# A gather of 1,563 tiles of rows: SyncE and ScalarE no longer fetch fifteen of them, GpSimd does

## The chip, the cores and the metric

The kernel runs on one core of a Trainium2 chip. The metric is the device time of one execution, in microseconds (us), as the median of several runs.

## What is computed

One layer of a graph network over N = 12,500 nodes with D = 256 features and E = 200,000 edges (src, dst), the edges sorted by dst:

```python
h = relu(layernorm(x))                      # per node, over 256 features
agg = segment_sum(h[src], dst, N)           # 200,000 gathered rows of 1 KB
t = ((1 + eps) * h + agg) @ W1 + b1         # W1 256 x 512
t = relu(batchnorm(t))                      # over all nodes
out = x + relu(batchnorm(t @ W2 + b2 + h))  # W2 512 x 256
```

All data are fp32.

## The kernel before

The edges are cut into 1,563 tiles of 128 (`TILES`), and these into 196 groups of `GT` = 8 (`NG`). For a tile, 128 rows of 1 KB are gathered from DRAM into 128 partitions; for a group, VectorE builds selection matrices (`selection`, `h_step`), and TensorE multiplies and sums them over the tiles of the group into a window of 96 nodes (`aggregate`, L1324). The window is copied, transposed and added into `aggT`.

In groups 0 to 29 (`H_FROM` = 30) the rows come from `x`, and VectorE and ScalarE normalise every gathered row (`statistics`, `normalise`). Beside this, all nodes are normalised once in batches of 512 and stored in DRAM as `h_rows`; from group 30 on the rows come from there and need no more work. Behind this, node tiles go through `z_tile` and `times_W1`. After the last group the kernel computes the first batch norm, multiplies by W2 (`times_W2`, L1442), computes the second batch norm, transposes back and adds x (`transpose_out`, L1456).

The order on each engine is written out by hand. GpSimd's program is a list of gathers, one indirect DMA for a tile (`gather`, L650):

```python
if g >= RG:
    pool.wait_ge(s_agg, g - RG + 1)      # RG = 4 buffers: group g - 4 must be aggregated
for k in range(tiles_of(g)):
    if sp_tile(g, k) or act_tile(g, k):
        continue
```

Fifteen tiles are left out there. SyncE fetches the last tile of groups 26, 54, 76, 96, 118, 140, 160 and 182 (`sp_groups`; group 26 from x), and ScalarE the last but one of groups 54, 75, 96, 118, 139, 160 and 182 (`act_groups`). Each does so with 128 DMAs of one row (`load_rows`, L512 and L1197), in pieces of 16, long before the group comes. For this each engine loads the byte offsets of the rows into registers. The offsets come from a table in DRAM (`row_at`): ScalarE multiplies the src table by 1,024 (L1078), SyncE stores it (L518), and GpSimd waits for that store (`s_atd`) before group 2, since the gathers' own table is made in the same place. Three buffers of rows for SyncE lie in `rl_odd`, three for ScalarE in `W2s`; therefore W2 is loaded only after ScalarE's last tile has been used (L566), and TensorE waits for it at L1433.

TensorE's wait at the head of a group (`wait_rows`) counts GpSimd's rows, and in the groups named also SyncE's and ScalarE's.

Of the kernel before, what the change touches and what calls it, by code (L numbers as in the profile page):

```python
# [39 lines left out]
SP_EIGHTHS = 6  # L40
ACT_EIGHTHS = 3
# [7 lines left out]
ROW_BUFS = 3  # L49
PIECE = 16  # L50
AT_ONCE = 32
QUAD = 4
ROW_BYTES = 4 * D


def ceil(a, b):
    return -(-a // b)


def build(nc, x, src, dst, W1, b1, g1, bt1, W2, b2, g2, bt2, eps_gin, out):  # L60
# [25 lines left out]
    with ctx:  # L86
# [6 lines left out]
        at_dram = nc.dram_tensor("row_at", (EB, P, P), i32, kind="Internal").ap()  # L93
        x_bytes = x.rearrange("n d -> (n d)").bitcast(mybir.dt.uint8)

        h_dram = nc.dram_tensor("h_rows", (N, D), f32, kind="Internal").ap()
        h_bytes = h_dram.rearrange("n d -> (n d)").bitcast(mybir.dt.uint8)
        H_ACT = H_FROM - 1

        def eighths(q, n):  # L100
            return q * n // 8

        per_tile = P // PIECE
        sp_groups = []
        while True:
            done = ceil(8 * per_tile * (len(sp_groups) + 1), SP_EIGHTHS)
            if done > H_NODES or 2 * (done - 1) + 6 >= H_FROM:
                break
            sp_groups.append(2 * (done - 1) + 6)
        SP_X = len(sp_groups)  # L110
        while True:
            done = ceil(8 * per_tile * (len(sp_groups) - SP_X + 1), SP_EIGHTHS) + H_NODES
            if 2 * (done - 1) + 6 >= NG - 4:
                break
            sp_groups.append(2 * (done - 1) + 6)

        act_groups = []
        while True:
            done = ceil(8 * per_tile * (len(act_groups) + 1), ACT_EIGHTHS) + H_ACT
            if done - 1 + 4 >= NG - 4:  # L120
                break
            act_groups.append(done - 1 + 4)

# [84 lines left out]
        assert COPIES_FROM % 2 == 1 and COPIES_FROM > max(H_ACT, 2 * H_NODES + 2, NQ + 2)  # L208
# [8 lines left out]
        sp_rows = [rl_odd[:, b * D:(b + 1) * D] for b in range(ROW_BUFS)]  # L217
        sp_at = [rl_odd[0:1, ROW_BUFS * D + b * P:ROW_BUFS * D + (b + 1) * P].bitcast(i32) for b in (0, 1)]
        w2_early = W2s.rearrange("p f d -> p (f d)")
        act_rows = [w2_early[:, b * D:(b + 1) * D] for b in range(ROW_BUFS)]  # L220
        act_at = [w2_early[0:1, ROW_BUFS * D + b * P:ROW_BUFS * D + (b + 1) * P].bitcast(i32) for b in (0, 1)]
# [40 lines left out]
        s_sprows = [sem(f"s_sprows{b}") for b in range(ROW_BUFS)]  # L262
        s_actrows = [sem(f"s_actrows{b}") for b in range(ROW_BUFS)]
        s_actat = [sem(f"s_actat{b}") for b in (0, 1)]
        s_spat = [sem(f"s_spat{b}") for b in (0, 1)]
        s_at, s_atd = sem("s_at"), sem("s_atd")
# [34 lines left out]
        def sp_tile(g, k):  # L301

            return g in sp_groups and k == GT - 1

        def act_tile(g, k):

            return g in act_groups and k == GT - 2

# [3 lines left out]

        def pool_tiles(g):

            return sum(not sp_tile(g, k) and not act_tile(g, k) for k in range(tiles_of(g)))
# [5 lines left out]
        def rows_of(g, k):  # L321
            if sp_tile(g, k):
                return sp_rows[sp_groups.index(g) % ROW_BUFS]
            if act_tile(g, k):
                return act_rows[act_groups.index(g) % ROW_BUFS]
            return rows[slot(g)][:, k, :]

        def row_pieces(first, end, tiles):

            return [divmod(n, P // PIECE) for n in range(first, min(end, tiles * P // PIECE))]  # L330

# [32 lines left out]
        def wait_rows(eng, g):  # L364

            eng.wait_ge(s_rows[g % RG], 16 * sum(pool_tiles(j) for j in range(g % RG, g + 1, RG)))
            if g in sp_groups:
                j = sp_groups.index(g)
                eng.wait_ge(s_sprows[j % ROW_BUFS], 16 * P * (j // ROW_BUFS + 1))
            if g in act_groups:  # L370
                j = act_groups.index(g)
                eng.wait_ge(s_actrows[j % ROW_BUFS], 16 * P * (j // ROW_BUFS + 1))

        def tiles_of(g):

            return min(GT, TILES - g * GT)
# [51 lines left out]
        def _(sp):  # L428
# [24 lines left out]
            sp.dma_start(W1s[:, :, :], W1.rearrange("(k p) n -> p k n", p=P)).then_inc(s_w, 16)  # L453

# [35 lines left out]
            def load_at(j):  # L490
                b, p = divmod(sp_groups[j] * GT + GT - 1, P)
                sp.dma_start(sp_at[j % 2], at_dram[b, p:p + 1, :]).then_inc(s_spat[j % 2], 16)

            row_regs = []

            def load_rows(j, m):
                if m == 0:
                    if j + 1 < len(sp_groups):
                        load_at(j + 1)
                    if j >= ROW_BUFS:  # L500
                        sp.wait_ge(s_agg, sp_groups[j - ROW_BUFS] + 1)
                    sp.wait_ge(s_spat[j % 2], 16 * (j // 2 + 1))
                if m * PIECE % AT_ONCE == 0:
                    regs = [sp.alloc_register(f"row{j}_{m}_{k}") for k in range(AT_ONCE)]
                    sp.reg_load(regs, sp_at[j % 2][0:1, m * PIECE:m * PIECE + AT_ONCE])
                    row_regs.extend(regs)
                for k in range(PIECE):
                    e = m * PIECE + k
                    reg = row_regs.pop(0)
                    at = sp.snap(reg, donate=True, min_val=0, max_val=(N - 1) * ROW_BYTES)  # L510
                    a = x_bytes if j < SP_X else h_bytes
                    sp.dma_start(sp_rows[j % ROW_BUFS][e:e + 1, :].bitcast(mybir.dt.uint8),  # L512
                                 a[bass.ds(at, ROW_BYTES)].rearrange("(p e) -> p e", p=1)
                                 ).then_inc(s_sprows[j % ROW_BUFS], 16)
                    sp.free_register(reg)

            sp.wait_ge(s_at, 1)
            sp.dma_start(at_dram.rearrange("b p e -> p b e"), tab_i[0]).then_inc(s_atd, 16)  # L518
            def pieces_of_pass(c):

                if c < H_NODES:
                    return row_pieces(eighths(SP_EIGHTHS, c), eighths(SP_EIGHTHS, c + 1), SP_X)
                c -= H_NODES
                return [(SP_X + j, m) for j, m in row_pieces(eighths(SP_EIGHTHS, c), eighths(SP_EIGHTHS, c + 1),
                                                            len(sp_groups) - SP_X)]

# [9 lines left out]
            for c in range(NT):  # L536
# [18 lines left out]
                if c == 0:  # L555
                    sp.wait_ge(s_trc[0], NTR)
                    sp.wait_ge(s_trc[1], NTR)
                    for b in (2, 3):
                        sp.dma_start(hb[b], batch_nodes(x, b, 0, P)).then_inc(s_pl[b], 16)
                    sp.wait_ge(s_atd, 16)  # L560
                    load_at(0)
                for j, m in pieces_of_pass(c):
                    load_rows(j, m)

            sp.wait_ge(s_agg, act_groups[-1] + 1)
            sp.dma_start(W2s[:, :, :], W2.rearrange("(k p) n -> p k n", p=P)).then_inc(s_w, 16)  # L566
# [53 lines left out]
        def _(pool):  # L620
# [11 lines left out]
            def gather(g):  # L632
                if g == PG:
                    pool.wait_ge(s_trc[1], NTR)
                    wait_apart(pool, s_trc[0], NTR)
                    wait_apart(pool, s_atd, 16)
# [4 lines left out]
                for k in range(tiles_of(g)):  # L641
                    if sp_tile(g, k) or act_tile(g, k):
                        continue
# [423 lines left out]
        def _(act):  # L1067
# [9 lines left out]
            act.wait_ge(s_tabf[0], 1)  # L1077
            S.activation(tab_i[0], tab_f[0], ACT.Copy, scale=float(ROW_BYTES)).then_inc(s_at, 1)  # L1078
# [97 lines left out]
            def load_at(j):  # L1176
                b, p = divmod(act_groups[j] * GT + GT - 2, P)
                act.dma_start(act_at[j % 2], at_dram[b, p:p + 1, :]).then_inc(s_actat[j % 2], 16)

            row_regs = []  # L1180

            def load_rows(j, m):
                if m == 0:
                    if j + 1 < len(act_groups):
                        load_at(j + 1)
                    if j >= ROW_BUFS:
                        act.wait_ge(s_agg, act_groups[j - ROW_BUFS] + 1)
                    act.wait_ge(s_actat[j % 2], 16 * (j // 2 + 1))
                if m * PIECE % AT_ONCE == 0:
                    regs = [act.alloc_register(f"act_row{j}_{m}_{k}") for k in range(AT_ONCE)]  # L1190
                    act.reg_load(regs, act_at[j % 2][0:1, m * PIECE:m * PIECE + AT_ONCE])
                    row_regs.extend(regs)
# [11 lines left out]
            def step(g):  # L1204
# [8 lines left out]
                if g == H_ACT:  # L1213
                    wait_h(act)
# [269 lines left out]
```

## Time and profile before

| What | Value |
|---|---|
| Median of 3 runs | 2167.27 us (2165.49 to 2168.1) |
| The profiled execution's own time | 2164.91 us |
| Its span, first to last instruction | 2163.1 us |
| GpSimd (POOL) busy | 1465.6 us, 68% of the span |
| TensorE (PE) busy | 1439.7 us, 67% |
| VectorE (DVE), ScalarE (ACT) busy | 769.0 and 338.3 us |
| Mean granted TensorE clock | 0.827 of full speed |
| DMA traffic | 324.90 MB, 150 GB/s over the span |

The own time is 1.81 us longer than the span: what lies around the instructions. Busy time leaves out the instructions that move registers, wait or issue a DMA on the hardware queues; a gather on GpSimd is counted for the part in which the engine works on it.

### The profile page before, as it was taken

What the parts mean: (1) busy time and instruction counts of PE and PEld (TensorE: products, weight loads), DVE (VectorE), ACT (ScalarE), POOL (GpSimd) and SP (SyncE); (2) the same over time, 40 slices, a digit from 0 to 9 for tenths busy, and PEclk for the clock granted to TensorE, in tenths of its full rate; (3) what the DMA queues carried; (4) which work ended last, traced back from release to release, by engine and by line L of the source; (5) the groups of instructions that cost most, each with busy time, mean ns of one, the idle gap of its engine ahead of it and who ended that gap; (6) DMA issues with size and microseconds to landing.
All of it is one profiled execution on the core that took longest, in us unless ns stands there. A gap on an engine that the chain in (4) does not pass through costs nothing.

```text
span 2163.1 us, 19306 instructions
## 1 busy us (share of the span) xinstructions
PE 1439.7 (67%) x4835; PEld 916.7 (42%) x4835; DVE 769.0 (36%) x1947; ACT 338.3 (16%) x661; POOL 1465.6 (68%) x1558
## 2 busy tenths in 40 slices
PE   3556667666665656575666575665666565689998
PEld 2334444444443434343444343433444343454446
DVE  7776753222322321322222222222232232134447
ACT  6667660000000000000000000000000000014446
POOL 7777777777777777777777777777777777760000
PEclk7788788787887877888778878888787788799999
DMA  6666654434434434434434443443443443448438
GB/s 201 214 226 213 223 170 128 138 109 135 137 108 135 135 116 128 135 115 128 136 115 125 138 122 119 135 136 106 135 135 106 135 134 115 144 126 320 178 139 317
DMA packets 119738, 324.90 MB, mean 150 GB/s; under 512 B 30146, under 2 KB 50939, under 8 KB 113487
## 3 DMA queue, kind: packets, MB, share of 16 engines
q0 software_dynamic: 74304, 203.00, 31.7%
q1 hardware_dynamic: 37036, 96.28, 12.5%
q10 hardware_dynamic: 8290, 24.43, 3.3%
q8 instruction: 38, 0.62, 0.1%
q14 instruction: 70, 0.57, 0.1%
HBM read 271.54 MB, written 52.05 MB: 150 GB/s over the span
## 4 chain that ended last, share of the span: by engine, by line
POOL 65%; issue 21%; PE 11%; DMA 1%; ACT 0%; DVE 0%; SPq 0%; DVEq 0%; POOLq 0%
POOL arena L650 65%; PE ps L1442 8%; PE ps L1456 1%; PE ps L1324 1%; DMA arena<-h_rows,arena 1%; PE ps L1360 0%; PE ps L1398 0%; DMA arena<-in_src 0%; DVE arena L1057 0%; SPq L439 0%; ACT aggT L1072 0%; ACT arena L1078 0%; ACT arena L1076 0%; PE ps L1334 0%; SPq L433 0%
## 5 line engine op out<-in xcount | busy, mean ns | idle before, releaser
L650 POOL DMA_INDIRECT arena<-h_rows,arena x1309 | 1237.4, 945 | 398.8 <-issue 397.9
L1324 PE MATMUL ps<-arena 128*96 128x256 f32 x3096 | 992.6, 491 | 688.2 <-DMA arena<-h_rows,arena 564.6
L1324 PEld LDWEIGHTS ps<-arena 128*96 128x96 f32 x3096 | 652.8, 217 | 1012.9 <-issue 748.4
L840 DVE TENSOR_TENSOR aggT<-aggT,ps 128x192 f32 x196 | 69.4, 354 | 1104.1 <-PE ps L1334 1101.7
L1151 ACT COPY arena<-ps 96x256 f32<-96x256 f32 x37 | 13.3, 358 | 1605.3 <-PE ps L1334 1570.0
L650 POOL DMA_INDIRECT arena<-in_x,arena x223 | 211.0, 946 | 67.9 <-issue 67.6
L1360 PE MATMUL ps<-arena 128*128 128x512 f32 (+3 forms) x412 | 186.3, 577 | 1.6 <-DVE arena L873 1.5
L1442 PE MATMUL ps<-arena,W2s 128*128 128x512 f32 (+1 forms) x400 | 167.9, 582 | 0.8 <-ACT arena L1272 0.8
L927 DVE TENSOR_TENSOR arena<-arena,ps 128x768 f32<-128x768 f32 x159 | 149.8, 942 | 0.0
L1103 ACT ACTIVATE arena<-arena,nb,mv 128x256 f32<-128x256 f32 x239 | 120.7, 587 | 84.5 <-DVE nb L744 84.5
L1442 PEld LDWEIGHTS ps<-arena,W2s 128*128 128x128 f32 x400 | 75.8, 190 | 92.8 <-issue 86.3
L676 DVE BATCH_NORM_STATS2 st<-arena 128x6 f32<-128x256 f32 x239 | 80.9, 411 | 58.6 <-DMA arena<-in_x,arena 58.5
L1360 PEld LDWEIGHTS ps<-arena 128*128 128x128 f32 x412 | 69.6, 190 | 48.1 <-issue 44.5
L924 DVE TENSOR_SCALAR arena<-ps,prmT 128x512 f32<-128x512 f32 x79 | 59.3, 751 | 75.9 <-PE ps L1360 75.9
L1272 ACT ACTIVATE arena<-arena,sh,sc 128x512 f32<-128x512 f32 (+1 forms) x100 | 72.1, 793 | 89.9 <-PE ps L1442 79.8
L1035 DVE SCALAR_TENSOR_TENSOR aggT<-ps,prmT,aggT 128x512 f32<-128x512 f32 (+1 forms) x50 | 36.9, 738 | 95.5 <-PE ps L1442 95.5
L1334 PEld LDWEIGHTS ps<-ident,arena 96*128 96x128 f32 x392 | 55.2, 142 | 26.5 <-ACT arena L1151 1.2
L918 DVE COPY arena<-ps 96x256 f32<-96x256 f32 x159 | 65.8, 414 | 0.1
L1334 PE MATMUL ps<-ident,arena 96*128 96x96 f32 x392 | 64.9, 246 | 0.6 <-ACT arena L1151 0.5
L881 DVE BATCH_NORM_STATS2 arena<-arena 128x6 f32<-128x512 f32 x92 | 63.0, 685 | 3.9 <-ACT arena L1160 3.9
L1117 ACT ACTIVATE arena<-arena,pnb,pmv 128x256 f32<-128x256 f32 (+1 forms) x100 | 51.7, 592 | 0.0
L934 DVE SCALAR_TENSOR_TENSOR arena<-ps,eps,aggT 128x256 f32<-128x256 f32 x80 | 38.1, 476 | 0.0
(99 smaller groups left out, 553.4 us busy)
## 6 DMA issues: line engine op xcount, KB each, us to landing
t_T<-arena SPq DMA_DIRECT2D x24, 1024.0 KB, 4.6
arena<-t_T SPq DMA_DIRECT2D x24, 1024.0 KB, 4.8
arena<-h_rows,arena POOLq DMA_INDIRECT x1309, 2.8
rl_odd<-h_rows SPq DMA_DIRECT2D x896, 1.0 KB
W2s<-h_rows ACTq DMA_DIRECT2D x896, 1.0 KB
arena<-in_x SPq DMA_DIRECT2D x27, 512.0 KB, 5.9
h_rows<-arena ACTq DMA_DIRECT2D x24, 512.0 KB, 3.7
out<-arena SPq DMA_DIRECT2D x23, 512.0 KB
```

The lines of the kernel that those rows point to most:

```text
L650: nc.gpsimd.indirect_dma_start(out=rows[slot(g)][:, k, :], out_offset=None, in_=(x if g < H_FROM else h_dram)[:, :], in_offset=bass.Indire ...
L676: last = V.bn_stats(o, r)
L840: V.tensor_tensor(z, z, winT_ps, ALU.add).then_inc(s_add, 1)
L881: V.bn_stats(o, t[:, m, :]).then_inc(s_tst, 1)
L918: V.tensor_copy(win_sb[g % 2], win_ps[g % 2]).then_inc(s_ev, 1)
L927: V.tensor_tensor(sel[:, g % 2, :, :], rel[:, g * GT:(g + 1) * GT].unsqueeze(2).to_broadcast([P, GT, W]), iota_ps.unsqueeze(1).to_broadcas ...
L1103: last = S.activation(rows_of(g, k), rows_of(g, k), ACT.Relu, bias=nb[:, g % 2, k:k + 1], scale=mv[:, g % 2, k, 1:2])
L1272: S.activation(u[:, k % 2, f, 0:n], tin[:, k % 2, f, 0:n], ACT.Relu, bias=sh1[:, f:f + 1], scale=sc1[:, f:f + 1]).then_inc(s_u, 1)
L1324: last = T.matmul(win_ps[g % 2], sel[:, g % 2, k, :], rows_of(g, k), start=k == 0, stop=k == n - 1)
L1334: last = T.transpose(winT_ps[:, f, :], win_sb[w % 2][:, f * P:(f + 1) * P], ident[0:W, 0:W])
L1360: last = T.matmul(t_ps[(FB * q + m) % TB][:, a:b], W1s[:, k, m * P:(m + 1) * P], zt[q % 2][:, k, a:b], start=k == 0, stop=k == DB - 1)
L1442: last = T.matmul(c_ps[k % 2][m][:, 0:n], W2s[:, f, m * P:(m + 1) * P], u[:, k % 2, f, 0:n], start=f == 0, stop=f == FB - 1)
```

## The change

The change takes out the fetches by SyncE and ScalarE with all that served them: the lists of groups, the offsets table and its store, the row buffers, their semaphores, and GpSimd's wait for `s_atd`. GpSimd gathers the fifteen tiles in their place in its order. W2 is loaded straight after W1, and TensorE waits for both before its first group. The waits of the remaining code are, as before, attached to the next instruction of their engine.

```diff
@@ wait_rows
-            eng.wait_ge(s_rows[g % RG], 16 * sum(pool_tiles(j) for j in range(g % RG, g + 1, RG)))
-            if g in sp_groups:
-                j = sp_groups.index(g)
-                eng.wait_ge(s_sprows[j % ROW_BUFS], 16 * P * (j // ROW_BUFS + 1))
-            if g in act_groups:
-                j = act_groups.index(g)
-                eng.wait_ge(s_actrows[j % ROW_BUFS], 16 * P * (j // ROW_BUFS + 1))
+            eng.wait_ge(s_rows[g % RG], 16 * sum(tiles_of(j) for j in range(g % RG, g + 1, RG)))
@@ SyncE
             sp.dma_start(W1s[:, :, :], W1.rearrange("(k p) n -> p k n", p=P)).then_inc(s_w, 16)
+            sp.dma_start(W2s[:, :, :], W2.rearrange("(k p) n -> p k n", p=P)).then_inc(s_w, 16)
...
-            sp.wait_ge(s_at, 1)
-            sp.dma_start(at_dram.rearrange("b p e -> p b e"), tab_i[0]).then_inc(s_atd, 16)
...
-                for j, m in pieces_of_pass(c):
-                    load_rows(j, m)
-
-            sp.wait_ge(s_agg, act_groups[-1] + 1)
-            sp.dma_start(W2s[:, :, :], W2.rearrange("(k p) n -> p k n", p=P)).then_inc(s_w, 16)
@@ GpSimd, gather
                     wait_apart(pool, s_trc[0], NTR)
-                    wait_apart(pool, s_atd, 16)
...
                 for k in range(tiles_of(g)):
-                    if sp_tile(g, k) or act_tile(g, k):
-                        continue
@@ ScalarE
             S.copy(tab_f[0], tab_i[0]).then_inc(s_tabf[0], 1)
-            act.wait_ge(s_tabf[0], 1)
-            S.activation(tab_i[0], tab_f[0], ACT.Copy, scale=float(ROW_BYTES)).then_inc(s_at, 1)
...
-                if g == H_ACT:
-                    wait_h(act)
-                if g >= H_ACT:
-                    for j, m in row_pieces(eighths(ACT_EIGHTHS, g - H_ACT), eighths(ACT_EIGHTHS, g - H_ACT + 1),
-                                           len(act_groups)):
-                        load_rows(j, m)
@@ TensorE
-            pe.wait_ge(s_w, 16)
+            pe.wait_ge(s_w, 32)
...
-            pe.wait_ge(s_w, 32)
```

GpSimd's list around group 54, before (a row is the group's first gather with its wait, or its other gathers; `arena` holds the gathered rows):

```order
L650 DMA arena<-h_rows,arena 128x256 x7
L650 DMA arena<-h_rows,arena 128x256 [waits s_agg]
L650 DMA arena<-h_rows,arena 128x256 x5
L650 DMA arena<-h_rows,arena 128x256 [waits s_agg]
L650 DMA arena<-h_rows,arena 128x256 x7
```

The same place now:

```order
L533 DMA arena<-h_rows,arena 128x256 x7
L533 DMA arena<-h_rows,arena 128x256 [waits s_agg]
L533 DMA arena<-h_rows,arena 128x256 x7
L533 DMA arena<-h_rows,arena 128x256 [waits s_agg]
L533 DMA arena<-h_rows,arena 128x256 x7
```

Group 54 had six gathers and has eight; where only SyncE or only ScalarE had a tile, x6 became x7.

SyncE's list at the outset, before (W1 and W2 both print as `in_L_gnn_W`):

```order
L452 DMA arena<-in_x 128x1024 x2
L453 DMA arena<-in_L_gnn_W 128x2x512
L518 DMA row_at<-arena 128x13x128 [waits s_at]
L460 DMA arena<-in_x 128x256
L559 DMA arena<-in_x 128x1024 [waits s_trc_dst,s_trc_src]
L559 DMA arena<-in_x 128x1024
L492 DMA rl_odd<-row_at 1x128 [waits s_atd]
```

The same place now:

```order
L380 DMA arena<-in_x 128x1024 x2
L381 DMA arena<-in_L_gnn_W 128x2x512
L382 DMA W2s<-in_L_gnn_W 128x4x256
L389 DMA arena<-in_x 128x256
L451 DMA arena<-in_x 128x1024 [waits s_trc_dst,s_trc_src]
L451 DMA arena<-in_x 128x1024
```

W2's load stands where the store of the offsets stood, and waits for nothing; the first node tile behind it no longer has a wait ahead of it.

## Rows read from the trace of the kernel before

**Rows 1.** The page, part 4: the chain of work that ended last.
```profile
POOL 65%; issue 21%; PE 11%; DMA 1%; ACT 0%; DVE 0%; SPq 0%; DVEq 0%; POOLq 0%
```
**Rows 2.** All gathers of line 650: durations (ns min/median/max), starts, idle time before.
```profile
L650 POOL DMA_INDIRECT arena<-h_rows,arena x1309: 942/946/958, 303.1 to 1938.1; - x187
L650 POOL DMA_INDIRECT arena<-in_x,arena x223: 942/946/1004, 24.2 to 301.9; - x112
L650 POOL DMA_INDIRECT arena<-in_x,idx x16: 942/946/1176, 3.8 to 22.9; - x16
...
  issue: 469.8, 1542
  DMA idx<-in_src: 1.3, 1
  PE ps L1324: 1.2, 4
  DVE arena L722: 0.3, 1
```
**Rows 3.** Busy time by stretch: start:end length, engines (instructions), PEclk, DMA share, GB/s.
```profile
600.00:800.00 200.00, 124.33 (x421) 81.30 (x422) 53.79 (x102) 0.00 (x0) 151.23 (x161) 0.81 0.41 122
...
1960.00:2020.00 60.00, 60.00 (x141) 26.60 (x140) 25.47 (x36) 26.36 (x36) 0.00 (x0) 1.00 0.75 280
```
**Rows 4.** Longest waits: who waited for whom, us in total, times, longest.
```profile
PE ps L1324 <- DMA arena<-h_rows,arena: 564.6, 147, 7.7
```
**Rows 5.** Timeline, the last gathers and the head of the tail.
```profile
1938.08 0.94 POOL L650 DMA_INDIRECT arena<-h_rows,arena  x1 [0.30 <-issue]
...
1952.32 4.10 PE L1442 MATMUL ps<-arena,W2s 128*128 128x512 f32 x9 [0.82 <-ACT arena L1272]
```
**Rows 6.** DMA issues: the row fetches (engine, operation, count, KB each).
```profile
rl_odd<-h_rows SPq DMA_DIRECT2D x896, 1.0 KB
W2s<-h_rows ACTq DMA_DIRECT2D x896, 1.0 KB
...
rl_odd<-in_x SPq DMA_DIRECT2D x128, 1.0 KB
```
**Rows 7.** Line 650 alone: POOL busy (count), PEclk, DMA share, GB/s by stretch.
```profile
559.00:609.00 50.00, 37.81 (x41) 0.83 0.47 140
...
682.00:732.00 50.00, 37.81 (x41) 0.80 0.37 105
```
**Rows 8.** Timeline, row fetches of ScalarE and SyncE in and around these stretches.
```profile
559.15 51.92 ACTq L1197 DMA_DIRECT2D W2s<-h_rows  x128
582.50 14.51 SPq L512 DMA_DIRECT2D rl_odd<-h_rows  x32
667.88 10.29 SPq L512 DMA_DIRECT2D rl_odd<-h_rows  x32
...
734.01 5.49 SPq L512 DMA_DIRECT2D rl_odd<-h_rows  x16
...
769.20 50.01 ACTq L1197 DMA_DIRECT2D W2s<-h_rows  x128
```
**Rows 9.** Timeline of the outset.
```profile
9.91 0.45 SPq L453 DMA_DIRECT2D arena<-in_L_gnn_W  x1
...
12.27 1.59 ACT L1078 ACTIVATE arena<-arena 128x1664 int32<-128x1664 f32 x1
...
13.88 0.38 SPq L518 DMA_DIRECT2D row_at<-arena  x1
...
15.16 7.25 DVE L704 COPY aggT<-ps 128x512 f32<-128x512 f32 x12
...
19.14 0.75 ACT L1083 CAST arena<-ps 128x512 int32<-128x512 f32 x2 [0.72 <-PE ps L1302]
...
22.34 2.69 DVE L676 BATCH_NORM_STATS2 st<-arena 128x6 f32<-128x256 f32 x8
...
24.18 0.94 POOL L650 DMA_INDIRECT arena<-in_x,arena  x1 [0.30 <-issue]
...
37.03 6.07 PE L1324 MATMUL ps<-arena 128*96 128x256 f32 x16 [3.85 <-issue]
```
**Rows 10.** DMA issues: the table's store, the load of W2.
```profile
row_at<-arena SPq DMA_DIRECT2D x1, 832.0 KB, 7.1
...
W2s<-in_L_gnn_W SPq DMA_DIRECT2D x1, 512.0 KB, 6.2
```
**Rows 11.** Timeline, the head of group 5.
```profile
48.22 5.60 PE L1324 MATMUL ps<-arena 128*96 128x256 f32 x16 [5.12 <-ACT arena L1103]
...
52.94 0.95 POOL L650 DMA_INDIRECT arena<-in_x,arena  x1 [0.30 <-issue]
...
54.19 0.95 POOL L650 DMA_INDIRECT arena<-in_x,arena  x1 [0.30 <-PE ps L1324]
```

More of the change, by code:

```diff
@@ L39 @@
 X_EARLY = 16
-SP_EIGHTHS = 6
-ACT_EIGHTHS = 3
 H_FROM = 30
@@ L48 @@
 HALF_G = GT // 2
-ROW_BUFS = 3
-PIECE = 16
-AT_ONCE = 32
 QUAD = 4
-ROW_BYTES = 4 * D
 def ceil(a, b):
@@ L91, in sem @@
             return ctx.enter_context(nc.semaphore(name))
-        at_dram = nc.dram_tensor("row_at", (EB, P, P), i32, kind="Internal").ap()
-        x_bytes = x.rearrange("n d -> (n d)").bitcast(mybir.dt.uint8)
         h_dram = nc.dram_tensor("h_rows", (N, D), f32, kind="Internal").ap()
[L97 to L122, printed above, removed]
         t_dram = nc.dram_tensor("t_T", (NQ, P, FB, QN), f32, kind="Internal").ap()
@@ L207, in build @@
         W1s = piece[1].rearrange("p (k n) -> p k n", n=F)
-        assert COPIES_FROM % 2 == 1 and COPIES_FROM > max(H_ACT, 2 * H_NODES + 2, NQ + 2)
+        assert COPIES_FROM % 2 == 1 and COPIES_FROM > max(H_FROM - 1, 2 * H_NODES + 2, NQ + 2)
         W2s = sb("W2s", [P, FB, D])
@@ L216, in build @@
         rl_odd = rl[1].rearrange("p f n -> p (f n)")
[L217 to L221, printed above, removed]
         mv1 = sb("mv1", [P, FB, 2])
@@ L261, in build @@
         s_half = [[sem(f"s_half{g}_{h}") for h in (0, 1)] for g in range(LAST)]
[L262 to L266, printed above, removed]
         s_pl = [sem(f"s_pl{b}") for b in range(HB)]
@@ L299, in wait_apart @@
             eng.sem_inc(s_apart, 1)
[L301 to L307, printed above, removed]
         def half_rows(g, k):
             return s_half[g - NG + LAST][k // HALF_G]
-        def pool_tiles(g):
-            return sum(not sp_tile(g, k) and not act_tile(g, k) for k in range(tiles_of(g)))
         def slot(g):
@@ L321, in rows_of @@
         def rows_of(g, k):
[L322 to L325, printed above, removed]
             return rows[slot(g)][:, k, :]
-        def row_pieces(first, end, tiles):
-            return [divmod(n, P // PIECE) for n in range(first, min(end, tiles * P // PIECE))]
         def batch_rows(b):
@@ L488, in load_x @@
                                  ).then_inc(s_x[k], 16)
[L490 to L515, printed above, removed]
-            sp.wait_ge(s_at, 1)
-            sp.dma_start(at_dram.rearrange("b p e -> p b e"), tab_i[0]).then_inc(s_atd, 16)
[L519 to L525, printed above, removed]
             def load_t(q, k, r, n=QN):
@@ L559, in _ @@
                         sp.dma_start(hb[b], batch_nodes(x, b, 0, P)).then_inc(s_pl[b], 16)
-                    sp.wait_ge(s_atd, 16)
-                    load_at(0)
-                for j, m in pieces_of_pass(c):
-                    load_rows(j, m)
-            sp.wait_ge(s_agg, act_groups[-1] + 1)
-            sp.dma_start(W2s[:, :, :], W2.rearrange("(k p) n -> p k n", p=P)).then_inc(s_w, 16)
             sp.wait_ge(s_add, NG)
@@ L1174, in _ @@
                 act.wait_ge(s_gend, 1)
[L1176 to L1192, printed above, removed]
-                for k in range(PIECE):
-                    e = m * PIECE + k
-                    reg = row_regs.pop(0)
-                    at = act.snap(reg, donate=True, min_val=0, max_val=(N - 1) * ROW_BYTES)
-                    act.dma_start(act_rows[j % ROW_BUFS][e:e + 1, :].bitcast(mybir.dt.uint8),
-                                  h_bytes[bass.ds(at, ROW_BYTES)].rearrange("(p e) -> p e", p=1)
-                                  ).then_inc(s_actrows[j % ROW_BUFS], 16)
-                    act.free_register(reg)
-            act.wait_ge(s_atd, 16)
-            load_at(0)
             def step(g):
```

## Prediction

> **What bounds the kernel now.** I read the chain of work that ended last first, then the gathers by their line, then the busy time by stretch, then the waits. The chain lies on GpSimd for 65% of the span, and another 21% is "issue" [rows 1]. The two belong together. There are 1309 + 223 + 16 = 1,548 gathers; each is busy for 0.946 us, and ahead of 1,542 of them lie 469.8 us of issue, 0.305 us each [rows 2]. The first starts at 3.8 us and the last at 1938.1 us, so 1,547 steps take 1934.3 us: **1.2503 us a gather**, from end to end of the list. In the same rows no gather waits for anything else for longer than this gap: the four that TensorE released had 1.2 us ahead of them in all, 0.3 us each, the one behind a VectorE copy 0.3 us, and only the very first waited for a DMA (1.3 us). GpSimd therefore never stands still between 3.8 and 1939.0 us, though its busy share reads 68%: the share misses the gap that comes with every gather.
>
> TensorE is busy for 124.33 of 200 us in the middle [rows 3], and what it waits for is the rows: 564.6 us in 147 waits [rows 4]. It follows GpSimd. The last gather starts at 1938.08 and ends at 1939.02 us [rows 5]; from there the kernel has 2163.1 - 1939.0 = 224.1 us of tail, in which TensorE is busy all of the time, at a granted clock of 1.00 [rows 3], first with W2 from 1952.32 us on [rows 5]. So the time is the sum of three pieces that do not overlap: 3.8 us until the first gather, the list of gathers, and the tail.
>
> **The fifteen tiles.** SyncE issues 896 + 128 rows and ScalarE 896 [rows 6], that is 8 + 7 = 15 tiles, and 1,548 + 15 = 1,563, the number of tiles of 128 in 200,000 edges. GpSimd now issues these 15 itself, in the middle of a list that has no hole: 15 x 1.2503 = **+18.75 us**. The bounds: the busy part alone would be 15 x 0.946 = 14.2 us, which nothing supports, since the gap stands ahead of every gather; the slowest gather on record, 1.176 us [rows 2], with its gap gives 15 x 1.48 = 22.2 us. I take the mean step, because 1,547 steps carry it and the new gathers stand among their like. Ten groups are touched: five had six gathers (7.5 us), five had seven (8.75 us), and all have eight now (10.0 us). TensorE, VectorE and ScalarE get more time for them, not less, so no wait comes from these groups.
>
> **What the other gathers gain.** The row fetches share the DMA engines with the gathers, so their going could quicken the rest. Two stretches of 50 us compare this. In 559 to 609 us ScalarE fetches almost throughout and SyncE for part; between 678 and 734 us neither fetches [rows 8]. GpSimd is busy for 37.81 us with 41 gathers in both, while the DMA share falls from 0.47 to 0.37 [rows 7]. I take 0. The other end: the fastest gather is 0.942 us against a median of 0.946 [rows 2]; were all like it, 1,563 x 0.004 = 6.3 us would be gained. As a slowing I allow the same.
>
> **The removed wait for the table's store, and the arithmetic for it.** GpSimd's wait for `s_atd` stands ahead of its seventeenth gather, at 24.18 us, which had nothing ahead of it but the gap [rows 9]. The store was issued at 13.88 us and took 7.1 us [rows 9, 10], so it had landed at 21.0. ScalarE's multiplication, 1.59 us at 12.27, goes too, and its table copies, finished by 19.9 us, come up to 1.6 us earlier; the gather that waits for them starts at 24.18 anyway [rows 9]. Gain: 0, hidden by the list of the first sixteen gathers.
>
> **W2 at the outset.** Its load goes out behind W1's, at 9.91 + 0.45 = 10.4 us. TensorE's first group starts at 37.03 us [rows 9]. W2 took 6.2 us late in the kernel, and the larger table 7.1 us at the crowded outset [rows 10]; landed by 18 us or, doubled, by 25 us, it is there 12 us before it is wanted. The outset moves 512 KB for W2 where it moved 832 KB for the table, but 3.5 us sooner, in front of the first node tile and beside the first gathers. Who would feel a late gather is VectorE, whose statistics start at 22.34 us right behind its own zeroing, which ran from 15.16 to 22.41 us [rows 9]: the rows of group 0 were already there, and VectorE and not a DMA set the pace. The place where this could reach GpSimd is group 5: its first gather needs group 1 aggregated, TensorE is done with that at 48.22 + 5.60 = 53.82 us, and GpSimd is free at 52.94 + 0.95 = 53.89 us [rows 11]. The slack is 0.07 us. I charge nothing, since the chain ahead of it (VectorE, ScalarE, TensorE) loses no cover; the upper bound is one landing of W2, 6.2 us. A gain is ruled out: GpSimd was already back to back there.
>
> **The tail, and the fetching engines.** The wait ahead of the products with W2 goes, and so does the late load. TensorE was held at 1952.32 us by ScalarE [rows 5], not by W2, so 0. SyncE and ScalarE lose 1,920 issues, none of which is on the chain (the SyncE queue has 0% of it, ScalarE 0% [rows 1]): 0. TensorE loses waits on up to two semaphores in the ten groups, whose rows had been fetched long before: 0.
>
> **The sum.** On the profiled execution's own time: 2164.91 + 18.75 = 2183.7 us. The median of the runs, 2167.27, is 2.36 us above that execution, and the run-to-run spread is 2.6 us; on the median the sum is 2167.27 + 18.75 = **2186.0 us**, and this I predict.
>
> **The rivals.** *One: nothing is lost, the data movement is the limit.* If the 16 DMA engines and not GpSimd's issuing paced the gathers, moving 1,920 rows of 1 KB from two queues to a third would cost nothing: 2167.3 us. For it: the gathers' 1,548 x 128 rows of 1 KB are 203 MB of the 325 MB moved. Against it: the DMA share is 0.41 in the middle [rows 3], and it changes by 0.10 between two stretches without moving GpSimd's step [rows 7]. The Trainium skill states a rule that leads here (DMA: Bandwidth & Descriptors, the section Issuing engines are not separate DMA queues): initiating DMAs on several engines at once saves only the time that a sequencer takes to initiate them, which is usually small beside the DMA itself. By that rule the forecast would be no change; the trace agrees with its first half and not with the "small", since 1.25 us of issuing per gather is the whole of the time up to 1939 us. Chance 0.03.
>
> *Two: faster than before.* GpSimd's step could shorten for all gathers once the single-row DMAs, their register moves and their semaphore updates are gone. It decides where the saving on 1,548 gathers passes 18.75 us: 12.1 ns each, a step of 1.238 us. At 15 ns it gives 2186.0 - 1,563 x 0.015 = 2162.6 us. Against it: the two stretches of rows 7 agree within 0.01 us in 37.81, and the fastest gather is only 4 ns below the median. Chance 0.02.
>
> *Three: slower still, through the outset.* W2's bytes delay a landing in front of group 1, and the 0.07 us of slack at group 5 is used up; every microsecond by which TensorE's 53.82 us moves beyond it is a microsecond of the whole list. With a full landing of 6.2 us: 2192.2 us. For it: the thin slack, and full DMA queues at the outset. Against it: VectorE was not waiting for rows there. Chance 0.07.
>
> That the change doesn't do what it says can be set aside: GpSimd's list shows the holes at the named groups filled.
>
> **How the numbers follow.** Forecast 0.88, rival one 0.03, two 0.02, three 0.07. About 0.2% (4.3 us) is what a measurement of this kernel can tell from no change. The forecast's own bounds are 2186.0 - 4.6 (busy part alone) and + 3.4 (slowest gather), so 2181.4 to 2189.4; the range is 2181 to 2190 us, and holds the forecast and the lesser part of rival three. Slower by over 0.2%: 0.88 + 0.07 = 0.95; within 0.2%: 0.03; faster: 0.02.
>
> **What would show it.** Right: 1,563 gathers with the same 0.946 us and 0.305 us of issue, the first at 3.8 us, the last at 1938.1 + 18.75 = 1956.8 us, and a tail of 224 us. Rival two would show in the step, rival three as idle time of GpSimd that TensorE ends near 54 us, rival one as a last gather still near 1938 us. The prediction is wrong if the first gather, the step or the tail moves by more than 1 us, 2 ns or 3 us.

## The result and the profile after

| | Before | After |
|---|---|---|
| Median | 2166.4 us (4 runs, 2165.49 to 2168.1) | 2184.2 us (4 runs, 2183.33 to 2184.74) |
| Own time of the profiled execution | 2164.91 us | 2184.31 us |
| Its span | 2163.1 us | 2182.2 us |
| First gather, last gather start | 3.76, 1938.08 us | 3.75, 1957.66 us |
| From the last gather's start to the end | 225.0 us | 224.5 us |

The changed kernel is slower by 17.8 us; the ratio is 1.0081, 95% interval 1.0063 to 1.0098. A fourth run of before had moved its median from 2167.27 to 2166.4 us.

The chain of work of the changed kernel, from part 4 of its page; it answers to [rows 1]:

```profile
POOL 65%; issue 21%; PE 11%; DMA 1%; DVE 0%; ACT 0%; POOLq 0%; DVEq 0%
```

All its gathers, the line now being 533; this answers to [rows 2]:

```profile
L533 POOL DMA_INDIRECT arena<-h_rows,arena x1323: 942/946/962, 304.9 to 1957.7; - x189
L533 POOL DMA_INDIRECT arena<-in_x,arena x224: 942/946/986, 24.7 to 303.7; - x112
L533 POOL DMA_INDIRECT arena<-in_x,idx x16: 942/946/1759, 3.7 to 23.5; - x16
...
  issue: 474.3, 1557
  PE ps L1171: 1.6, 5
  DMA idx<-in_src: 1.2, 1
```

1323 + 224 + 16 = 1,563 gathers, with the same median of 0.946 us and the same gap (474.3 us / 1,557 = 0.305 us). The list took 1957.66 - 3.75 = 1953.9 us against 1934.3, **19.6 us more**; the rest of the kernel took 0.5 us less. Fifteen steps of 1.2503 us are 18.75 us of it. The other 0.8 us has two places that can be seen, both at the outset. The first is the third row's maximum: one gather took 1.76 us where the longest before took 1.18. The timeline of the changed kernel shows it, beside VectorE's conversion of the dst table and SyncE's new load of W2:

```profile
10.09 1.03 DVE L601 CAST arena<-arena 128x1664 f32<-128x1664 int32 x1 [2.52 <-DMA arena<-in_dst]
10.17 1.76 POOL L533 DMA_INDIRECT arena<-in_x,idx  x1 [0.30 <-issue]
10.30 0.84 SPq L382 DMA_DIRECT2D W2s<-in_L_gnn_W  x1
```

That is 0.58 us. The second is the head of group 5, which answers to [rows 11]:

```profile
48.09 6.44 PE L1171 MATMUL ps<-arena 128*96 128x256 f32 x16 [5.94 <-ACT arena L984]
...
53.50 0.95 POOL L533 DMA_INDIRECT arena<-in_x,arena  x1 [0.30 <-issue]
...
54.80 0.95 POOL L533 DMA_INDIRECT arena<-in_x,arena  x1 [0.35 <-PE ps L1171]
```

TensorE ended group 1 at 54.53 us and GpSimd was free at 54.45, so GpSimd waited 0.05 us longer than the gap. This is the thin place of the prediction: group 1 took TensorE 6.44 us in place of 5.60. The two delays overlap: without the long gather GpSimd would have been free at 53.87 us and would still have waited for TensorE's 54.53, so the first gather of group 5 would have started at the same 54.80 us, 0.61 us later than before. What differed at group 1 is the clock granted to TensorE, over 48 to 55 us 0.59 after and 0.70 before. W2 at the outset is not needed for this: the kernel with 35 tiles further down has the outset of the kernel before, its granted clock there was 0.64, group 1 took 6.00 us, and group 5 waited 0.35 us beyond the gap:

```profile
54.52 0.94 POOL L650 DMA_INDIRECT arena<-in_x,arena  x1 [0.65 <-PE ps L1324]
```

Why the clock differed between these executions is open. The remaining 0.2 us is spread over 1,500 steps. W2's load was seen to land after 9.1 us, at 19.4 us, and TensorE's first group began at 36.95 us, as before.

### The profile page after: what moved, and what is told of

Read it like the earlier page. It is cut to its first block, busy times and chain, and to the rows that moved or that the text cites. A ratio compares the mean times of both kernels' runs of the same rounds, so it can differ in the third digit from the quotient of the medians.

```text
span 2182.2 us, 15375 instructions
## 1 busy us (share of the span) xinstructions
PE 1445.3 (66%) x4835; PEld 922.4 (42%) x4835; DVE 769.0 (35%) x1947; ACT 336.9 (15%) x660; POOL 1480.7 (68%) x1573
## 4 chain that ended last, share of the span: by engine, by line
POOL 65%; issue 21%; PE 11%; DMA 1%; DVE 0%; ACT 0%; POOLq 0%; DVEq 0%
POOL arena L533 65%; PE ps L1287 8%; PE ps L1301 1%; PE ps L1171 1%; DMA arena<-h_rows,arena 1%; ACT arena L984 0%; PE ps L1245 0%; PE ps L1207 0%; DVE st L559 0%; DVE arena L940 0%; POOLq L80 0%; ACT arena L1119 0%; DVE aggT L944 0%; DVE mv L566 0%; DVEq L80 0%
## 5 line engine op out<-in xcount | busy, mean ns | idle before, releaser
L533 POOL DMA_INDIRECT arena<-h_rows,arena x1323 | 1250.9, 946 | 403.0 <-issue 401.8
L1171 PE MATMUL ps<-arena 128*96 128x256 f32 x3126 | 1003.8, 492 | 701.8 <-DMA arena<-h_rows,arena 574.3
L1171 PEld LDWEIGHTS ps<-arena 128*96 128x96 f32 x3126 | 662.6, 218 | 1028.5 <-issue 763.3
L810 DVE TENSOR_TENSOR arena<-arena,ps 128x768 f32<-128x768 f32 x159 | 149.8, 942 | 0.0
L639 DVE TENSOR_TENSOR arena<-arena,ps 128x768 f32<-128x768 f32 x37 | 35.0, 946 | 8.8 <-PE ps L1171 8.8
```

What stands on the lines that cost most here:

```text
L533: nc.gpsimd.indirect_dma_start(out=rows[slot(g)][:, k, :], out_offset=None, in_=(x if g < H_FROM else h_dram)[:, :], in_offset=bass.Indire ...
L810: V.tensor_tensor(sel[:, g % 2, :, :], rel[:, g * GT:(g + 1) * GT].unsqueeze(2).to_broadcast([P, GT, W]), iota_ps.unsqueeze(1).to_broadcas ...
L1171: last = T.matmul(win_ps[g % 2], sel[:, g % 2, k, :], rows_of(g, k), start=k == 0, stop=k == n - 1)
```

## The experiments

The theory: up to 1939 us the kernel's time is GpSimd's list, one step of 1.25 us for every tile that it gathers, and row fetches by other engines neither slow nor quicken this step. The rivals: the movement of data sets the pace; the step depends on the other engines' fetches; W2 at the outset has a price. Each ratio is against the kernel before, measured beside it on the same chip.

**W2's load back at the end of SyncE's loop**, in the changed kernel:

```diff
-            sp.dma_start(W2s[:, :, :], W2.rearrange("(k p) n -> p k n", p=P)).then_inc(s_w, 16)
             def load_node_tile(c, n=P):
...
+            sp.dma_start(W2s[:, :, :], W2.rearrange("(k p) n -> p k n", p=P)).then_inc(s_w, 16)
             sp.wait_ge(s_add, NG)
...
-            pe.wait_ge(s_w, 32)
+            pe.wait_ge(s_w, 16)
...
+            pe.wait_ge(s_w, 32)
```

TensorE waits for W1 alone at the outset again, and for W2 before its products with it.

> The changed kernel with W2's load put back behind SyncE's loop, as before the change; nothing else differs. Theory (W2's load at the outset lengthens the sixth gather and nothing else): the sixth gather, 1.76 us in the changed kernel and 1.18 us before, is back at 1.2 us, group 5 starts with the bare gap again, the last gather starts about 0.6 us earlier (1957.0 us), and the own time is 0.6 us below 2184.3. Rival (the longer gather has another cause, such as VectorE's conversion of the table that runs beside it in both kernels): it stays at 1.7 us and nothing changes. Rival (W2 at the outset pays off in the tail): the tail behind the last gather grows from 223.6 to over 224 us.

Measured: 2184.33 us, before 2165.4 us, ratio 1.0088 (1.0071 to 1.0105). The theory on W2 fell. The sixth gather stayed long, though less so, with no W2 near it:

```profile
9.91 1.03 DVE L601 CAST arena<-arena 128x1664 f32<-128x1664 int32 x1 [2.34 <-DMA arena<-in_dst]
10.18 1.57 POOL L533 DMA_INDIRECT arena<-in_x,idx  x1 [0.30 <-issue]
```

The last gather started at 1957.37 us, and the span's rest behind it was 2182.0 - 1957.4 = 224.6 us, against 224.5. W2's place is worth nothing at either end.

**ScalarE's seven tiles to GpSimd, SyncE's eight kept**, in the kernel before:

```diff
         act_groups = []
-        while True:
-            done = ceil(8 * per_tile * (len(act_groups) + 1), ACT_EIGHTHS) + H_ACT
...
-            act.wait_ge(s_atd, 16)
-            load_at(0)
```

> The kernel before with ScalarE's seven tiles given to GpSimd, SyncE's eight left. Theory (each tile costs one step of 1.2503 us on GpSimd's list, whoever fetched it): 1,555 gathers, 7 x 1.25 = 8.8 us above before, 2175.2 us. Rival (ScalarE's fetches had a price or gain of their own, so the loss is not in proportion): the last gather does not start at 1938.1 + 8.8 = 1946.9 us, or the time is off by more than 2 us.

Measured: 2174.14 us against 2165.4, ratio 1.0037 (1.0023 to 1.0052): 8.7 us for seven tiles. The last of 1,555 gathers started at 1947.28 us, against 1946.9 expected. The cost is in proportion to the number of tiles.

**Fifteen tiles fetched by SyncE and ScalarE, waited for, and not used**, GpSimd gathering all:

```diff
-            return sum(not sp_tile(g, k) and not act_tile(g, k) for k in range(tiles_of(g)))
+            return tiles_of(g)
...
-            if sp_tile(g, k):
-                return sp_rows[sp_groups.index(g) % ROW_BUFS]
-            if act_tile(g, k):
-                return act_rows[act_groups.index(g) % ROW_BUFS]
             return rows[slot(g)][:, k, :]
...
-                    if sp_tile(g, k) or act_tile(g, k):
-                        continue
```

> The kernel before, with SyncE and ScalarE still fetching their 15 tiles and everybody still waiting for them, while GpSimd gathers all 1,563 tiles and only its rows are used. Theory (row fetches neither slow GpSimd's step nor are slowed by it): as the changed kernel, step 1.250 us, last gather at 1957 us, 2184 to 2186 us. Rival two (the step gets quicker without the row fetches): a step above the changed kernel's, by 12 ns if the whole 18.75 us were to be cancelled, thus up to 2203 us. Rival one (data movement sets the pace): 1,920 more rows of 1 KB, 1% more gathered bytes, about 19 us above the changed kernel.

Measured: 2184.65 us, ratio 1.0086 (1.0069 to 1.0102). The gathers of this kernel, by line:

```profile
L644 POOL DMA_INDIRECT arena<-h_rows,arena x1323: 942/946/962, 304.8 to 1957.6; - x189
```

With 1,920 more row DMAs than the changed kernel, with the offsets' table, its store and GpSimd's wait for it, the gathers of h rows run from 304.8 to 1957.6 us; in the changed kernel from 304.9 to 1957.7. Rivals one and two are excluded here, and the removed store, wait and arithmetic are shown to have cost nothing. What counted was how many tiles GpSimd gathers.

**More tiles for SyncE and ScalarE.** Five counts, each the kernel before with two constants changed, as here for 35 tiles:

```diff
-SP_EIGHTHS = 6
-ACT_EIGHTHS = 3
+SP_EIGHTHS = 12
+ACT_EIGHTHS = 8
```

> The other way: the kernel before with 35 tiles fetched by SyncE and ScalarE in place of 15 (16 and 19), so that GpSimd gathers 1,528. Theory (the list sets the time as long as the fetched rows are there in time): 20 x 1.25 = 25 us below before, 2141.4 us, last gather at 1913.1 us. Rival (SyncE's or ScalarE's queue becomes late: a piece of 16 rows takes SyncE 5.1 us, and stores and loads of the node work stand behind it): idle time of GpSimd ended by TensorE, which waits for the fetched rows, and less than 25 us gained.

Measured: 2141.15 us, ratio 0.9886 (0.987 to 0.9903), 24.3 us below before, the last gather at 1913.84 us.

For 51 and 62 tiles (16 and 12, 24 and 12) the first runs fell on a chip on which the kernel before itself took 2474 us:

> The kernel before with 51 tiles fetched by SyncE (22) and ScalarE (29), so that GpSimd gathers 1,512. Theory (the list alone sets the time while rows are there in time): 36 x 1.25 = 45 us below before, 2120.4 us, last gather at 1893 us. ScalarE needs 1.5 pieces of 16 rows in a group's 10 us, about 0.39 us a row: 9.4 us, nearly all of its time. Rival (ScalarE's queue falls behind, and TensorE waits for its rows): GpSimd idle before gathers, ended by TensorE, and a time above 2123 us.

> As the one before, but SyncE takes 33 tiles and ScalarE 29; GpSimd gathers 1,501. Theory: 47 x 1.25 = 58.8 us below before, 2106.7 us. SyncE then spends 3 x 5.1 = 15.4 of the 20 us of a pass on rows, beside its stores and loads. Rival (a queue or TensorE becomes the bound): idle time of GpSimd ended by TensorE, and the gain over the 51 tiles is under 11 x 1.25 = 13.8 us.

They gave 3085.95 and 3241.27 us. There GpSimd's own gathers kept their 0.945 us, but several engines had long gaps ahead of instructions that the profile puts down to nothing in the kernel; why that chip did so is open, and nothing is drawn from it. Both ran again:

> Run f1_51_tiles over again, since on the chip of that call the kernel before itself took 2474 us, 309 us more than in the calls ahead of it. Same expectations: by the list alone 2120.4 us, last gather at 1893 us; by the rival a time above 2123 us with GpSimd idle until TensorE, which waits for ScalarE's rows.

> Run f2_62_tiles over again. By the list alone 2106.7 us; by the rival less than 13.8 us below the 51 tiles, with idle time of GpSimd ended by TensorE.

With 51 tiles: 2148.19 us, ratio 0.9893 (0.9877 to 0.991), 22.4 us below before where the list alone would give 45. With 62: 2256.47 us, ratio 1.0392 (1.0375 to 1.041). The bound has moved. The chain of the kernel with 51 tiles, part 4 of its page:

```profile
ACTq 52%; POOL 18%; issue 16%; PE 11%; DMA 1%; ACT 0%; DVE 0%; SPq 0%; DVEq 0%; POOLq 0%
```

and ScalarE's queue beside it on the timeline, one tile from its first row to the next tile's:

```profile
1011.13 51.30 ACTq L1197 DMA_DIRECT2D W2s<-h_rows  x128
1062.47 0.29 ACTq L1178 DMA_DIRECT2D W2s<-row_at  x1
1065.13 14.87 ACTq L1197 DMA_DIRECT2D W2s<-h_rows  x36
```

A tile costs ScalarE 1065.13 - 1011.13 = 54 us. GpSimd passes the 5.33 groups between two of its tiles in 5.33 x 8 = 42.7 gathers less 1.7 fetched, 41 x 1.25 = 51 us. (The expectation had put ScalarE's row at 0.39 us, just enough; with the load of the offsets it is 54 / 128 = 0.42 us.) ScalarE is late by 3 us a tile, and TensorE waits for it:

```profile
PE ps L1324 <- DMA W2s<-h_rows: 349.7, 19, 29.0
```

GpSimd in turn waits for TensorE 17 times, 25.6 us in all, most of them late in the list. That is 20 us beyond the usual gaps. From the last gather's start to the end it takes 2146.4 - 1918.8 = 227.6 us, 2.6 us more than before; together this accounts for the 22.6 us by which the gain falls short.

With 62 tiles the chain is SyncE's (41% of the span). TensorE waits 246.4 us for SyncE's rows, and VectorE 417.2 us for the store of t, which stands behind SyncE's row fetches in its list:

```profile
DVE arena L924 <- DMA t_T<-arena: 417.2, 16, 34.5
```

From these 54 us came the last two kernels, 41 tiles (16 and 8) and 46 (16 and 10):

> 22 tiles by SyncE, 19 by ScalarE; GpSimd gathers 1,522. In the run with 51 tiles ScalarE needed 54 us for a tile (51.3 us for 128 rows, and the load of the next offsets), while GpSimd passed the 5.33 groups between two of its tiles in 51 us: so ScalarE was late. Here it has 8 groups, 77 us. By the list: 26 x 1.25 = 32.5 us below before, 0.985 of its time. If SyncE were late with 22 tiles: GpSimd idle until TensorE and less gained.

> 22 tiles by SyncE, 24 by ScalarE; GpSimd gathers 1,517. ScalarE has 6.4 groups for a tile, 62 us against its 54: in time. By the list: 31 x 1.25 = 38.8 us below before, 0.982 of its time. If 54 us is too low a price for ScalarE's tile: late as with 51 tiles, and slower than the 41 tiles.

Measured: 41 tiles, 2135.9 us, ratio 0.9856 (0.9839 to 0.9872); **46 tiles, 2127.86 us, ratio 0.9818 (0.9801 to 0.9834)**, before 2167.4 us. Both as the list gives it, and 46 tiles is the fastest of all versions. Its gathers:

```profile
L650 POOL DMA_INDIRECT arena<-h_rows,arena x1280: 942/946/962, 301.1 to 1900.3; - x183
...
  issue: 458.4, 1503
  PE ps L1324: 4.0, 12
```

All versions side by side, each against before on its own chip:

| Tiles by SyncE + ScalarE | GpSimd gathers | List gives | Measured |
|---|---|---|---|
| 0 (the change) | 1,563 | +18.8 us | +17.8 us |
| 0 (W2 late; rows unused) | 1,563 | +18.8 | +18.9; +19.3 |
| 8 + 0 | 1,555 | +8.8 | +8.7 |
| 16 + 19 | 1,528 | -25.0 | -24.3 |
| 22 + 19 | 1,522 | -32.5 | -31.5 |
| 22 + 24 | 1,517 | -38.8 | -39.5 |
| 22 + 29 | 1,512 | -45.0 | -22.4 |
| 33 + 29 | 1,501 | -58.8 | +85.9 |

**One more copy on VectorE in every second group**, in the changed kernel, to explain the long sixth gather:

```diff
             def h_step(g):
+                if g % 2 == 0:
+                    V.tensor_copy(rl_odd[:, 0:1024], rel[:, 0:1024])
```

> The changed kernel with one more copy on VectorE in every second group from group 33 on, 128 x 1024 fp32 from SBUF to SBUF, whose result nobody uses: some 80 copies. In all runs so far the gather that ran beside VectorE's conversion of the dst table from SBUF to SBUF was longer than 0.946 us (1.18 to 1.76 us), the more of it the earlier the conversion began, and no gather beside VectorE's other work was; the load of W2 has no part in it. Theory (a copy within SBUF on VectorE holds GpSimd's gather up while it runs): some 80 gathers stretched by 0.2 to 0.9 us each, 15 to 70 us on the time, the last gather at 1973 to 2028 us. Rival (the long sixth gather comes from the burst of loads at the outset): all gathers stay at 0.946 us and the time stays at 2184 us, since VectorE is idle for three quarters of this stretch.

This run was on the chip with the long gaps too (2475.73 us), and was made again:

> Run g1_vector_copies over again: by the theory some 80 gathers stretched by 0.2 to 0.9 us each, last gather at 1973 to 2028 us, 15 to 70 us above the changed kernel's 2184.2; by the rival all gathers at 0.946 us and 2184 us. In the disturbed run the h gathers' mean was 959 ns against 946, 13 ns x 1,323 = 17 us in all, 0.2 us a copy; that is what I now expect, 2201 us.

Measured: 2200.18 us, before 2170.57 us, ratio 1.0131 (1.0114 to 1.0148). On this chip the gathers have a median of 0.949 us, so the changed kernel would be at about 2170.6 + 18.8 = 2189.4 us (worked out, not run there), and the 79 copies cost some 11 us. That is less than the 15 to 70 us expected, and less than the 17 us of the last estimate; the 2201 us was met by luck, since it was reckoned from 2184.2 us and this chip is slower. That the copies lengthen gathers is borne out by the trace:

```profile
L533 POOL DMA_INDIRECT arena<-h_rows,arena x1323: 945/949/1418, 305.7 to 1973.7; - x189
```

The longest gather of h rows went from 0.962 to 1.418 us. In the timeline, 63 of the gathers that overlap one of these copies took over 0.965 us, 11.6 us above 0.949 together. Three copies show that the order matters, columns as before:

```profile
340.55 0.68 DVE L797 COPY rl_odd<-arena 128x1024 f32<-128x1024 f32 x1
340.77 1.28 POOL L533 DMA_INDIRECT arena<-h_rows,arena  x1 [0.30 <-issue]
...
397.66 0.95 POOL L533 DMA_INDIRECT arena<-h_rows,arena  x1 [0.31 <-issue]
397.73 0.68 DVE L797 COPY rl_odd<-arena 128x1024 f32<-128x1024 f32 x1
...
434.00 1.20 POOL L533 DMA_INDIRECT arena<-h_rows,arena  x1 [0.30 <-issue]
434.06 0.43 DVE L823 COPY aggT<-ps 128x256 f32<-128x256 f32 x1
434.40 0.68 DVE L797 COPY rl_odd<-arena 128x1024 f32<-128x1024 f32 x1
```

A copy that was running when the gather began cost it 0.33 us; one that began 0.07 us behind the gather's start cost nothing; one that began 0.40 us behind it cost 0.25 us. The rival, that the burst of loads makes gathers long, does not explain 63 long gathers between 340 and 1974 us.

## Why the prediction was right

**The bound and its step.** Right. The chain, the median gather, the gap and the count came as forecast, and the count was varied from 1,517 to 1,563 with the time following at 1.25 us each.

**The sum.** The forecast of 2186.0 us was 1.8 us above the median. The term of 18.75 us was sound: the list grew by 19.6 us and the span by 19.1. The weaker term was the base. I added to 2167.27 us, a median of three in which the profiled execution's 2164.91 did not count; from that execution's own time the sum was 2183.7, and its counterpart came at 2184.31. On three other chips before stood at 2165.4, 2167.4 and 2170.6 us. Executions on one chip differ by 2 us too, and behind the list: the profiled one with the unused rows took 2186.77 us where the median is 2184.65, with its last gather at the usual 1957.6 us and 227.2 us from there to the end, against 224.5. So an agreement of the medians closer than 2 us is luck. The prediction also says of the tail that TensorE is busy for all of it, from rows that cover 60 of its 224 us; in the last 63 us it is busy for 56.7. Nothing in the sum hangs on that.

**What the other gathers gain: 0.** Right, and now shown by the run with unused rows, not only by two stretches of 50 us.

**The wait for the table's store and the arithmetic: 0.** Right; that same run had all of it and the same gathers.

**W2 at the outset: 0.** Right in size. It landed by 19.4 us, within the 18 to 25 us allowed, and its late load gave the same time. The reason given for the sixth gather's length in [rows 2] was none: I took its 1.176 us as the tail of a spread. It is an overlap with a conversion on VectorE, and moved to 1.76 us because the two began 0.08 us apart the other way round. Why it begins earlier or later from run to run is open; without W2 at the outset it began anywhere from 9.91 to 10.65 us. This 0.58 us was not in the sum, nor was the wait at group 5, where the slack of 0.07 us was named.

**The rivals.** One (data movement) and two (a quicker step) are excluded. Three (a delay through the outset) was there in kind, 0.6 us of it: TensorE's end of group 1 did move past the slack, by its granted clock, and no run shows W2 to have a part in it. The rule of the Trainium skill weighed under rival one (DMA: Bandwidth & Descriptors, Issuing engines are not separate DMA queues), that issuing from several engines saves only a usually small sequencer time, has to be read from its first half: what it saves is issue time, and here issue time is the kernel. Its other side showed at 51 tiles, where ScalarE's issue time, 54 us a tile, became the bound.

## What to carry to other kernels

Where an engine's instructions follow one another at an even step, count them and multiply, and do not read the busy share: GpSimd was at its limit with 68%. A helper that takes work off such a list was worth its share in full here, up to 46 tiles, and has a limit of its own that can be worked out ahead: price per tile (54 us) against the time that the list takes between two of its tiles. Stay a little below that, since one late helper stops the engines behind it: 46 tiles gained 39.5 us, 51 only 22.4.

## What had not been expected

A copy or a conversion from SBUF to SBUF on VectorE lengthens a gather on GpSimd that runs beside it, and when the gather ends depends on which of the two began first.

The sixth gather took 1.76, 1.57 and 1.67 us where the conversion had begun 0.08 to 0.27 us before it. It then ended 0.81 or 0.82 us behind the conversion's end: 11.93 - 11.12 in the changed kernel, 11.75 - 10.94 with W2 late. It took 1.18 us where the conversion of 1.06 us began with it (to 0.01 us), and 1.58 us where it began 0.43 us behind it. In these two it ended only 0.12 us behind the conversion's end: 11.37 - 11.25 before, 11.80 - 11.68 with SyncE's tiles alone. So it is not "the earlier the conversion, the longer the gather", as the expectation of the copies has it.

The 79 copies follow the same two patterns in the timeline:

- In 44 cases the copy was running when a gather began. The gather ended 0.81 to 0.82 us behind the copy's end, and took 1.02 to 1.42 us.
- In the other 35 the copy began 0.02 to 0.50 us into the gather. The gather ended 0.12 us behind the copy's end where that was later than its own 0.95 us, and lost nothing where it was not.
- In 29 of the 44 the copy had begun 0.55 us or more into the gather ahead. That gather kept its 0.95 us, and where the copy had begun 0.55 to 0.77 us into it, the copy took longer, up to 0.92 us in place of 0.68.

The Trainium skill has this (SBUF — State Buffer, section SBUF: two separate sides): VectorE and GpSimd share a pair of ports, which whoever starts first holds for the whole instruction, and GpSimd cannot write DMA descriptors while VectorE copies fp32 within SBUF. The trace agrees for a copy that was there first. It agrees only in part for one that starts during a gather: up to 0.50 us into it the copy went ahead (the copy at 434.40 us cost the gather 0.25 us), and from 0.55 to 0.77 us the copy was held.

Beside VectorE's batch-norm work in groups 0 to 29 single gathers were long too, up to 1.06 us; this was not followed up.
